# A rule that spaces TensorE's side products out, zero-valued products in the first slots, and one transpose moved from slot 1 to slot 2

## What is computed

```
x = layernorm(x + attention_0(x))     # 16 heads of 8; q and k scaled to unit length; a temperature per head
x = layernorm(x + ffn_0(x))           # x rounded to int8 by rows, one 128 x 128 product, a bias
x = layernorm(x + attention_1(x))     # 16 heads of 8; q and k layer-normed and rotated; causal mask
x = layernorm(x + ffn_1(x))           # silu(x Wg) * (x Wu), then Wd; hidden size 384
```

## Time and profile before

| | us |
|---|---|
| median of three runs | 831.9 |
| the profiled execution, its own time | 833.45 |
| its span, first to last instruction | 831.4 |
| ACT busy in the span | 772.3 |
| PE busy in the span | 803.6 |
| DVE busy in the span | 540.3 |
| POOL busy in the span | 169.9 |

### The profile page before, as it was taken

The page is one execution under the profiler, slowest core; times in us unless marked ns, Lnnn a source line. Parts: engine busy times, 40 slices in busy tenths (PEclk is TensorE's granted clock), DMA queues, the critical chain, the costliest instruction groups (busy, mean ns, idle before and its releaser), DMA issues.

```text
span 831.4 us, 18912 instructions
## 1 busy us (share of the span) xinstructions
PE 803.6 (97%) x7457; PEld 295.6 (36%) x7457; DVE 540.3 (65%) x1426; ACT 772.3 (93%) x869; POOL 169.9 (20%) x370
## 2 busy tenths in 40 slices
PE   8899999999999999999999999999999999999996
PEld 4223332333333433343333433343333343443444
DVE  4265666868867787876663677675754267785656
ACT  4899999999999999999999999999999999898972
POOL 3110000100000601033000611023200354362220
PEclk9899999999999999999999999999999999999999
DMA  5765414242602631362130421321231231071000
GB/s 144 248 225 190 177 40 146 83 141 76 242 27 88 231 140 39 99 232 78 59 133 26 150 81 39 140 90 45 72 130 51 81 110 51 27 240 53 15 14 15
DMA packets 48556, 88.74 MB, mean 107 GB/s; under 512 B 5200, under 2 KB 14544, under 8 KB 48464
## 3 DMA queue, kind: packets, MB, share of 16 engines
q1 hardware_dynamic: 47696, 85.95, 30.4%
q0 software_dynamic: 288, 1.05, 0.4%
q10 hardware_dynamic: 480, 0.48, 0.2%
HBM read 50.50 MB, written 35.65 MB: 104 GB/s over the span
## 4 chain that ended last, share of the span: by engine, by line
PE 75%; ACT 13%; DVE 7%; issue 3%; DMA 0%; ACTq 0%; DVEq 0%
PE ps L1011 37%; PE ps L989 21%; ACT probs L826 13%; PE ps L879 9%; PE ps L868 3%; PE ps L964 3%; DVE th L1421 1%; DVE hT L1422 1%; PE ps L873 1%; PE ps L1045 1%; PE ps L1053 0%; DVE sums_t L1249 0%; DVE gate_sb L1416 0%; DVE mid_part L1411 0%; DVE mid_part L1412 0%
## 5 line engine op out<-in xcount | busy, mean ns | idle before, releaser
L826 ACT ACTIVATE probs<-ps 128x1024 f32<-128x1024 f32 x800 | 749.3, 1057 | 31.0 <-PE ps L989 21.2
L1011 PE MATMUL ps<-probs,v_st 128*32 128x512 f32 (+3 forms) x3584 | 428.1, 560 | 3.2 <-issue 2.4
L989 PE MATMUL ps<-q_st,k_st 32*128 32x512 f32 (+3 forms) x1792 | 266.3, 460 | 7.8 <-ACT probs L826 7.2
L989 PEld LDWEIGHTS ps<-q_st,k_st 32*128 32x128 f32 x1792 | 120.1, 182 | 288.0 <-ACT probs L826 221.7
L734 POOL TENSOR_SCALAR_AFFINE_SELECT probs<-probs 128x256 f32<-128x256 f32 x256 | 103.8, 428 | 144.7 <-ACT probs L826 143.0
L1011 PEld LDWEIGHTS ps<-probs,v_st 128*32 128x32 f32 x3584 | 78.7, 108 | 110.4 <-issue 74.2
L702 POOL COPY v_st<-v_all 128x256 f32<-128x256 f32 (+1 forms) x65 | 29.1, 456 | 343.2 <-PE ps L1011 334.9
L1249 DVE STREAM_TRANSPOSE sums_t<-ps 128x512 f32<-128x512 f32 x32 | 22.9, 716 | 45.3 <-PE ps L1011 44.7
L1390 DVE COPY mid_qkv<-ps 128x384 f32<-128x384 f32 x32 | 17.8, 557 | 35.8 <-PE ps L879 34.8
L964 PE MATMUL ps<-yTp,w_hid 128*128 128x512 f32 x84 | 31.2, 453 | 4.1 <-DVE gate_sb L1416 2.5
L1390 DVE COPY prep_qkv<-ps 128x384 f32<-128x384 f32 x24 | 13.4, 558 | 27.1 <-PE ps L879 26.4
(11 more groups left out here) (190 smaller groups left out, 641.3 us busy)
## 6 DMA issues: line engine op xcount, KB each, us to landing
k_st<-parts_scratch SPq DMA_DIRECT2D x46, 512.0 KB, 3.6
parts_scratch<-mid_part SPq DMA_DIRECT2D x34, 512.0 KB, 4.4
q_st<-parts_scratch SPq DMA_DIRECT2D x62, 256.0 KB, 3.9
parts_scratch<-prep_part SPq DMA_DIRECT2D x28, 512.0 KB, 4.8
k_st<-parts_scratch SPq DMA_DIRECT2D x17, 256.0 KB, 2.9
xT<-in_xT SPq DMA_DIRECT2D x8, 256.0 KB, 4.4
x_all<-in_x SPq DMA_DIRECT2D x8, 256.0 KB, 5.3
out<-yo SPq DMA_DIRECT2D x7, 256.0 KB, 2.3
```

The lines of the kernel that those rows point to most:

```text
L826: nc.scalar.activation(probs[:, k % PS, :, 0:w], slot(k)[:, :, 0:w], ACT.Exp).then_inc(probs_ready, 1)
L989: last_ = mm(slot(k)[:, e, at:at + n], k_st[row, p % KB, kt * P:(kt + 1) * P], q_st[row, p % KB, lo:HALF], start=True, stop=not shifted)
L1011: last_ = mm(acc[HR * h:HR * (h + 1), lo:HALF], v_st[:, p % VB, kt, h, :], probs[:, (2 * s + h // 2) % PS, h % 2, at:at + n], start=FIRST[ ...
```

## The change

Three edits.

1. In the planner, a unit is not placed in slot s when slot s - 1 has one on TensorE, unless the job is late. Late is reckoned as s plus the slots that the rest of the job needs (1.0 for each unit on TensorE, 0.6 for each piece on VectorE) being at or past `due`. The rule holds ahead of the last 60 slots. `proj` is placed in its fixed slot as before and does not ask the rule.
2. In the first slots, two products of zeros follow each `scores(k)` for k from 3 to 6. They write ACC, which nothing uses until `sums(0)` starts its sum there. `BETWEEN` is allowed only from slot 7 on.
3. The transpose of q of the second chunk moves from slot 1 to slot 2.

```
+def slots_left(j):
+    return sum(REST if e == "pe" else 0.6 for e, what, k in UNITS[j["name"]][j["n"]:])      # REST = 1.0
...
-    out[1] += FIRST_KEYS[1:]
+    out[1] += FIRST_KEYS[1:2]
+    out[2] += FIRST_KEYS[2:]
...
-            if s < NS - 1 and max(one, act) + 0.45 < sums - GAIN:
+            if BRANCHED <= s < NS - 1 and max(one, act) + 0.45 < sums - GAIN:
                 between.add(s)
...
             if not fits(j, pe + (SLACK if s < NS - END else LATE)):
                 continue
+            if s < NS - END and any(x[2] == "pe" for x in out[s - 1]) and s + slots_left(j) < j["due"]:
+                continue
             out[s].append((name, c, e, what, k))
...
-    WARM = (10, 4, 0, 22)
+    WARM = (10, 4, 0, 22, 7)
...
                     if k % 2 and s in BETWEEN:
                         sums(s - 1)
+                    if k < WARM[4]:
+                        keep_warm(2, ACC)
```

More of the change, by code:

```diff
@@ L296, in side_order @@
     return out, jobs, front, between
-SLACK, LATE, OVER, TURN_BY, END, FREE, AHEAD, GAIN = 0.2, 1.5, 1.6, 1.6, 60, 3, 0.0, -0.2
+SLACK, LATE, OVER, TURN_BY, END, FREE, AHEAD, GAIN, REST = 0.2, 1.5, 1.6, 1.6, 60, 3, 0.0, -0.2, 1.0
 SIDE_ORDER, JOBS, FRONT, BETWEEN = side_order()
```

## The result

The changed kernel takes 827.04 us (median of 3 runs, 826.14 to 827.36) against 831.9 us: a ratio of 0.9931, interval [0.9917, 0.9946]. It is faster by 4.9 us, where 12.4 were forecast. The profiled execution took 827.04 us itself, its span is 825.0 us, against 833.45 and 831.4 us before.

A forecast was written before the change was run, and what follows sets the result against it. ScalarE's back-to-back exponentials set a floor of 1.81 us a slot, with 33.7 us lost against it. Spacing 8.9 plus start 3.5 gave 12.4 us: 819.5 us against the 831.9 median, 8-in-10 range 813.5 to 828.

The forecast's parts named there:

- the start: First slots: zeros in TensorE's pauses keep the clock at 1.0, exponentials 7 and 8 on pace; 3.5 us won.
- The rule of long idle gaps: Start's clock: only a long idle gap between matmul bursts lowers it, so zeros change nothing; no chance of its own.
- the price of a lone `qkv`: `qkv` with an empty slot behind it: ScalarE loses 0.08 us, bounded by 0 and 0.25.
- the rule's sum: Slots beside units: spacing them cuts ScalarE's loss from 30.2 to 21.3 us, 8.9 us won.
- part 1: The spacing rule's step: no unit added or removed, TensorE's, DVE's and ScalarE's work stays; gain 8.9 us.
- The 9.0 us for light neighbours: Loss before the change left to 57 light units with a neighbour, 0.16 us each, a remainder without its own row.
- the likeliest case: The forecast itself, whole kernel: 12.4 us won, 819.5 us, own range 816 to 823.5; chance 0.55.
- Spacing wins nothing: Rival, beside units: heavy ones cost 0.25 us and light ones 0.16 wherever they stand; only start won, 828.4 us; chance 0.14.
- Slower, by units ahead of the sums: Rival, 64 more slots: sums wait behind a unit, next scores behind both; lone units cost 0.28 us, 836.7 us; chance 0.06.
- Lone units are free: Rival, beside lone units: TensorE catches up wholly, 4.6 us more won, 814.9 us; chance 0.17.
- the clock falls all the same: Rival, at the start: 3.5 us not won, up to 3.6 added, 823.0 to 826.6 us; chance 0.08.
- The second fall: Near 754 us, clock at 0.5 again: this fall may go or another join, 2.2 us either way.

The follow-up runs named there:

- both shortenings: Changed kernel with three of four operations of mid's second rsqrt step left out and seven transposes' split second half cut to 32 columns: 823.1 us, 0.9894.
- the start alone: Changed kernel without the spacing rule, keeping the zeros in the first slots, the limit on `BETWEEN` and the moved transpose: 829.83 us, 0.9962 of the kernel before.
- kernel of later dues: Changed kernel with mid's small operations priced at 0.33 us and later due slots, so fewer jobs count as late: 823.54 us, 0.9901 of the kernel before.
- with the price: Changed kernel with the planner pricing mid's small VectorE operations at 0.33 us instead of 0.21: 824.64 us, 0.9908 of the kernel before.
- the units behind the sums: Changed kernel with units up to slot 340 placed behind their slot's sums, except at a turn: 832.66 us, 1.0004 of the kernel before.
- the last one: Kernel of later dues, plus no elementwise piece of a job in the two slots behind a group's end: 822.6 us, 0.9878 of the kernel before.

## Why the prediction was right and wrong

**Right: the start.** 3.1 of 3.5 us; the missing 0.4 are small losses in slots 3 and 4 (0.15 and 0.21 us), where sums and the moved transpose crowd in, which I had costed at nothing. Wherever zeros were in, the clock of the start read 1.0, in all eleven profiles of such kernels; in the three without them it fell to 0.5 for 6.83 us. The rule of long idle gaps, which I carried as a rival by the Trainium skill ("TensorE: Matmul & The Clock Gate", section "Why this matters for your kernels"), does not explain this place: pauses of 0.42 us preceded the fall, and it went when they were filled. The zeros, the moved transpose and the limit on `BETWEEN` were tried only together; that it was the zeros is not shown by itself.

**Right: the price of a lone `qkv`.** 0.07 us, the median of 35, against 0.08 from one row. The bounds 0 and 0.25 were not needed. The sum over lone units still came out at +5.5 instead of +3.8 us: lone light units were priced at 0.04 from two transposes, but `normT` and `gate` cost 0.16 and 0.12 (medians), and five `qkv` cost 0.16 to 0.63.

**Wrong: the rule's sum, 8.9 us, of which 1.7 came.** The step that failed is in part 1, the forecast's wait on VectorE, which it put at nothing: prices per unit were read in the order before and carried into another one, with `proj` kept at 3.6 us and "In `FRONT` slots ... covered, if only just" as the only word on what a unit waits for. I priced units by their neighbours on TensorE alone. That TensorE's, VectorE's and ScalarE's work stays says nothing about the order in which VectorE gets it. The spaced units meet VectorE at other moments: behind mid's small operations, which the planner has too cheap, and, as transposes, in front of the turn that `proj` needs. The runs show 2.3 us for the first and 2.05 for the second, 4.55 together, and nothing for the first on the kernel before (the second was not tried there, but there no `proj` up to slot 340 had such a pause ahead of it). With both, VectorE ends 1.5 us of TensorE's pauses in slots 5 to 340 instead of 4.8. Of the 7.2 us that the rule fell short, 4.55 is the larger part.

**The rest, 2.7 us, is read from the ledger and not shown by a run:** with both shortenings, `proj` costs what it did before (6.8 and 6.9), neighbours fell by 11.3 where 12.7 were forecast, and lone units rose by 5.5 instead of 3.8. The 9.0 us for light neighbours was a remainder, as I said there, and it was too large: by the ledger neighbours cost 23.1 us before, where the prediction had 16.8 + 9.0, and the slots around `proj` 6.9, where it had 3.6 from one lone `proj`. (The plan has 59 and 37 light units with a neighbour, not 57 and 35; the difference of 22 is the same.)

**The rivals.** The time lies within the range, up to 828, but not in the 816 to 823.5 us of the likeliest case; that the range took it in is luck, since half of a rival that did not hold had been added to it. By its middle value "Spacing wins nothing" came nearest in time (828.4) and is wrong as a mechanism: units with a neighbour gave back 9.6 us. "Slower, by units ahead of the sums" had it upside down: that order is worth about 3 us of the 4.4 measured. "Lone units are free" is out (they cost 5.5 us more), and so is "the clock falls all the same" (it read 1.0).

**The second fall.** The prediction held 2.2 us either way for it, tied to the order at 754 us. It is rather a matter of the execution: the kernel of both shortenings took 822.4 and 822.8 us at a mean clock of 0.999 and 823.4 and 824.0 at 0.995 and 0.996; the start alone 828.0 us at 0.999 and 829.8 to 830.3 at 0.995 to 0.997. (The kernel of later dues does not follow this: 823.0 us at 0.998, 823.5 and 823.6 at 0.999.) So the 1.6 us that the profile of the changed kernel shows from slot 341 on can't be put to the change.

## What to carry to other kernels

A price of a piece of work that is read beside its neighbours on one engine holds only as long as the engine that hands over its buffer is early; when an order is changed, go through each moved piece's releaser in the new order, above all where that engine's queue also holds something that another fixed step needs. An order that is planned from a cost table shifts its errors about: first compare the table's prices with the rows (0.21 against 0.33 us here). And filling short pauses with products of zeros can be cheap where a fall of the clock follows them: eight of them came with 3.1 us here.

## What the runs showed of the hardware that was not expected

- The clock fell for one stretch of 3.4 us at quite different places in these kernels (754 us before, 317 with the price, 706 with the units behind the sums, 744 in the last one) and in some executions not at all; where it lies behind slot 340, the slots from 341 on lose 16.0 to 16.7 us, without it 15.0 to 15.2. It had no one place in the code.
- A VectorE operation on 128 x 128 values takes 0.29 us and 0.33 from start to start; cutting one from 512 to 32 columns saved 0.69 - 0.19 = 0.50 us.
- Pauses of TensorE in slots 5 to 340 add up to 9.3 us before and 9.0 after, nearly alike. What changed is who ends them: a pause that ScalarE ends is free there, a pause that VectorE ends comes back as idle time of ScalarE (0.55 us and 0.54 at slot 94).
- VectorE and GpSimd were slow side by side: four VectorE operations on 128 x 128 values took 2.12 us instead of 0.87 beside a GpSimd addition of 1.28 us, and two GpSimd maskings 1.75 us instead of 0.77 beside a VectorE multiplication of 1.67 us (at 393.80 us in the changed kernel). No run was made on it.
